# A new order of pieces for a four-part transformer kernel, with an earlier start of batch 0's query rows and paired expert products

## What is computed

```python
x = x + L0_attn(_layernorm(x))   # 16 heads of 8, softmax over 256 keys, relative tables rel_k, rel_v clipped at +-20
x = x + L0_ffn(_layernorm(x))    # rmsnorm; per token: attention of 16 heads over each other (low-rank k, v);
                                 # rmsnorm; softmax gate over 8 experts, each one 128x128 product
x = x + L1_attn(_layernorm(x))   # rmsnorm; linear attention, 8 heads of 16, second-order Taylor features
x = x + L1_ffn(_layernorm(x))    # top-2 of 8 experts + a shared one: silu((x w1 + b1)(x w3 + b3)) w2 + b2, hidden 176
```

## Time and profile before

| | us |
|---|---|
| median of 3 runs (all: 812.59, 813.42, 817.56) | 813.42 |
| the profiled execution | 821.41 |
| its span, first to last instruction | 819.6 |
| PE busy in it | 671.8 (82%) |
| DVE busy | 567.0 (69%) |
| ACT busy | 393.2 (48%) |
| POOL busy | 153.0 (19%) |
| mean granted clock of PE | 0.937 |

### The profile page before, as it was taken

How to read it: one execution, slowest core, us unless ns; L and a number is a source line. 1 busy time by engine, 2 the same in 40 slices (tenths; PEclk the granted TensorE clock), 3 DMA queues, 4 the chain that set the end, 5 groups by cost and what they waited for, 6 DMA issues and landing times.

```text
span 819.6 us, 16984 instructions
## 1 busy us (share of the span) xinstructions
PE 671.8 (82%) x6432; PEld 532.3 (65%) x6432; DVE 567.0 (69%) x1482; ACT 393.2 (48%) x953; POOL 153.0 (19%) x179
## 2 busy tenths in 40 slices
PE   2377772887799899989998999889998995877886
PEld 1256651775587678767886688668876773656655
DVE  3122178458876997699769985998589857787174
ACT  1164333544565556555556555665565453324241
POOL 2311120412040205030403041202221102011000
PEclk9998885999799999999999999999999999699799
DMA  2701100110011001100110011001100010000000
GB/s 69 253 2 14 14 7 0 15 16 7 1 15 15 7 1 21 15 7 2 20 15 8 1 20 16 8 1 21 15 1 2 8 14 0 2 7 0 1 8 6
DMA packets 75958, 13.45 MB, mean 16 GB/s; under 512 B 69851, under 2 KB 74981, under 8 KB 75749
## 3 DMA queue, kind: packets, MB, share of 16 engines
q1 hardware_dynamic: 75314, 10.84, 7.4%
q0 software_dynamic: 384, 1.05, 0.4%
q10 hardware_dynamic: 180, 0.48, 0.2%
...
## 4 chain that ended last, share of the span: by engine, by line
PE 39%; issue 34%; DVE 12%; ACT 6%; POOL 3%; SPq 3%; DMA 2%; POOLq 0%; ACTq 0%
PE bank L1026 5%; PE bank L1047 4%; PE bank L1224 4%; PE bank L1065 3%; PE bank L1225 3%; PE bank L1145 3%; DVE nmx L725 2%; PE bank L1089 2%; PE bank L1036 2%; ACT pm L451 2%; POOL q3h L602 2%; PE bank L1178 1%; SPq L373 1%; SPq L349 1%; PE bank L965 1%
## 5 line engine op out<-in xcount | busy, mean ns | idle before, releaser
L451 ACT ACTIVATE pm<-bank,nmx 128x256 f32<-128x256 f32 x256 | 100.5, 475 | 126.3 <-DVE nmx L725 126.3
L725 DVE TENSOR_REDUCE nmx<-bank 128x2 f32<-128x512 f32 x128 | 82.3, 684 | 72.7 <-PE bank L1036 72.6
L1047 PE MATMUL bank<-w,pm 128*128 128x128 f32 x512 | 84.5, 291 | 29.6 <-ACT pT L459 24.4
L1026 PE MATMUL bank<-kT,qbd 64*64 64x256 f32 x1024 | 90.7, 417 | 13.2 <-issue 12.9
L459 ACT ACTIVATE pT<-bank 128x512 f32<-128x512 f32 x128 | 77.2, 603 | 38.1 <-PE bank L1047 37.9
L1047 PEld LDWEIGHTS bank<-w,pm 128*128 128x128 f32 x512 | 63.7, 151 | 42.7 <-ACT pm L451 30.5
L934 DVE SCALAR_TENSOR_TENSOR hu<-bank,w,ha 128x256 f32<-128x256 f32 x104 | 50.1, 482 | 53.3 <-ACT ha L516 52.9
L1065 PE MATMUL bank<-tv,pT 128*128 128x128 f32 (+1 forms) x512 | 84.7, 284 | 0.0
L1065 PEld LDWEIGHTS bank<-tv,pT 128*128 128x128 f32 x512 | 75.0, 202 | 3.5 <-issue 2.1
L516 ACT ACTIVATE ha<-bank,w 128x256 f32<-128x256 f32 x104 | 49.7, 478 | 55.1 <-PE bank L1225 54.2
L1224 PE MATMUL bank<-xfT,w 128*128 128x256 f32 x208 | 66.6, 402 | 8.5 <-DVE hu L934 8.5
...
## 6 DMA issues: line engine op xcount, KB each, us to landing
...
```

Source lines behind the costliest of these rows:

```text
L451: a = act.activation(pm[:, s % 2, c, j], b_s[c][:, j * S:(j + 1) * S], exp, bias=nmx[:, i:i + 1])
L725: v.tensor_reduce(nmx[:, i:i + 2], b_s[c][:].rearrange("p (j k) -> p j k", j=2), AX_X, ALU.max, negate=True).then_inc(max_ready[0], 1)
L1026: mm(b_s[c][cols:cols + P // 2, j * S:(j + 1) * S], qbd[rows:rows + P // 2, i], kT[rows:rows + P // 2, t % 2, u], start=True, stop=False, ...
L1047: a = nc.tensor.transpose(b_t[:, (j * 2 + kc) * P:(j * 2 + kc + 1) * P], chunk(pm[:, s % 2, c, j], kc), ident)
```

## The change

- batch 0's row projection of q goes into bank b_b ahead of q^T and k^T, DVE adds its bias in project0, and v goes into b_a without waiting for kT;
- relkT and relv are loaded first; DVE fills only ek, ahead of norm0, and ACT fills ev; SP makes eight shifted copies (three before d_ev, five after), and one transfer copies them to the other 64 partitions; ACT issues the second half of qc for batch 0, DVE makes one of the first two qr blocks, and w's second part waits for qc;
- moments uses bn_aggr; tanh and the product behind it take two chunks at a time (the last one alone);
- x1 has two buffers, lsum shares lmx and y shares xl;
- every piece but the scores has a new position, and the order is computed by a sort (DRIFT is 0).

```diff
+HPAIRS = (NCH + 1) // 2
...
-PREPARE_AT = [-337, -315, -287, -256, -179, -62, 15]
+PREPARE_AT = [-352, -331, -274, -259, -93, 0, 12]
...
-ATTENTION_AT = [0, 60, 120, 180, 240, 300, 360, 420, 41, 65, 93, 109, 168, 184, 194, 254, 257, 281, 347, 358, 406, 428, 438,
-                454, 70, 129, 155, 184, 202, 232, 258, 273, 319, 345, 375, 395, 429, 444, 463, 466, 188, 296, 404, 468, 213,
-                74, 485, 501, 528, 543, 537, 548, 553, 579]
+ATTENTION_AT = [0, 60, 120, 180, 240, 300, 360, 420, 29, 74, 103, 142, 175, 185, 206, 225, 272, 278, 336, 379, 399, 416, 434,
+                446, 122, 128, 180, 191, 209, 219, 245, 245, 313, 315, 396, 408, 424, 440, 457, 463, 191, 289, 416, 467, 55,
+                24, 471, 491, 525, 550, 535, 551, 572, 585]
...
-FEED_AT = [589, 609, 611, 639, 652, 660, 663, 667, 670, 674, 680, 682, 685, 690, 690, 695, 701, 704, 714, 723, 723, 733,
-           734, 736, 736, 749, 761, 767, 768, 827, 852, 877, 905, 926, 973, 1005]
+FEED_AT = [585, 592, 602, 611, 626, 643, 652, 662, 664, 670, 673, 673, 673, 684, 699, 704, 707, 713, 718, 740, 741, 743,
+           759, 774, 781, 813, 816, 840, 855, 882, 907, 910, 920, 946, 958, 963]
...
-SECOND_AT = [1031, 1044, 1076, 1147, 1153, 1164, 1169, 1175, 1176, 1196, 1206, 1214, 1215, 1215, 1215, 1218, 1218, 1224,
-             1246, 1252]
+SECOND_AT = [974, 1031, 1059, 1088, 1112, 1141, 1156, 1173, 1175, 1177, 1192, 1220, 1221, 1227, 1236, 1257, 1268, 1274,
+             1303, 1358]
...
-LATE_AT = [1282, 1307, 1308, 1350, 1396, 1419, 1443, 1454, 1470, 1492, 1511, 1546, 1552, 1591, 1613, 1617, 1621, 1644,
-           1650, 1676, 1688, 1697, 1727, 1743]
+LATE_AT = [1360, 1366, 1378, 1392, 1408, 1427, 1436, 1442, 1475, 1527, 1555, 1579, 1597, 1630, 1638, 1657, 1659, 1660,
+           1675, 1701, 1733, 1760, 1800, 1812]
...
+DRIFT = 0
+STEP = [PERIOD + (DRIFT if k >= len(PREPARE + ATTENTION) else 0) for k in range(len(ALL))]
 PIECES = sorted([(at, k, piece) for k, (piece, at) in enumerate(zip(ALL, ALL_AT))])
+TURNS = [(t, piece) for _, _, _, t, piece in sorted([(t * STEP[k] + at, at, k, t, piece) for at, k, piece in PIECES for t in range(B)])]
...
-        x1 = sb("x1", P, C, E)
+        x1 = sb("x1", P, 2, C, E)
...
-        lsum = sb("lsum", P, C, H0)
+        lsum = lmx
...
-        y = sb("y", P, C, E)
+        y = xl
...
+        def own_rows(half):
+
+            src = bass.AP(d_qdh.tensor, half * D0, [[H0, QI * D0], [QI * D0 * H0, RT], [1, D0]])
+            return qc[half * QI * D0:(half + 1) * QI * D0], src
...
-            sp.wait_ge(rel_filled[0], 1)
-            for half in range(2):
-                for qi in range(QI):
-                    p0 = (half * QI + qi) * D0
-                    sp.dma_start(tk[p0:p0 + D0, :], ek[0:D0, QI - 1 - qi:QI - 1 - qi + TKN]).then_inc(tk_in[0], 16)
-            sp.wait_ge(rel_filled[0], 2)
+            def shifted(first, last):
+
+                for qi in range(first, last):
+                    sp.dma_start(tk[qi * D0:(qi + 1) * D0, :], ek[0:D0, QI - 1 - qi:QI - 1 - qi + TKN]).then_inc(tk_in[0], 16)
+
+            sp.wait_ge(ek_filled[0], 1)
+            shifted(0, 3)
+            sp.wait_ge(ev_filled[0], 1)
             sp.dma_start(d_ev.rearrange("m d -> (m d)").rearrange("(a n) -> a n", a=1)[:, TV0 * D0:], ev[0:1, TV0 * D0:]).then_inc(ev_out[0], 16)
+            shifted(3, QI)
             sp.wait_ge(ev_out[0], 16)
...
+                if t == 0:
+                    sp.wait_ge(tk_in[0], 16 * QI)
+                    sp.dma_start(tk[QI * D0:], tk[0:QI * D0]).then_inc(tk_copied[0], 16)
                 sp.wait_ge(*raised(qdh_out, t, 16))
                 sp.wait_ge(*raised(qr_ready, t, 0))
-                for half in range(2):
-                    src = bass.AP(d_qdh.tensor, half * D0, [[H0, QI * D0], [QI * D0 * H0, RT], [1, D0]])
-                    sp.dma_start(qc[half * QI * D0:(half + 1) * QI * D0], src).then_inc(qc_in[0], 16)
+                if t == 1:
+                    sp.wait_ge(qr0_ready[0], 1)
+                for half in range(2 if t else 1):
+                    sp.dma_start(*own_rows(half)).then_inc(qc_in[0], 16)
...
+            sp.wait_ge(qc_in[0], 32)
...
-            act.dma_start(r[:], rpack.partition_broadcast(P)).then_inc(r_in[0], 16)
             act.dma_start(ek[0:D0, S - REL + QI - 1:S + REL + QI], relkT).then_inc(rel_in[0], 16)
             act.dma_start(ev[0:1, (S - 1 - REL) * D0:(S + REL) * D0], relv).then_inc(rel_in[0], 16)
+            act.dma_start(r[:], rpack.partition_broadcast(P)).then_inc(r_in[0], 16)
             act.dma_start(b2s[:], b2).then_inc(small_in[0], 16)
...
+            def fill_ends():
+
+                act.wait_ge(rel_in[0], 32)
+                lo, hi = S - 1 - REL, S + REL
+                act.activation(view(hu, TV0 * D0, [[D0, lo - TV0], [1, D0]], 0, 1), view(hu, lo * D0, [[0, lo - TV0], [1, D0]], 0, 1), copy)
+                act.activation(view(hu, hi * D0, [[D0, EV - hi], [1, D0]], 0, 1),
+                               view(hu, (hi - 1) * D0, [[0, EV - hi], [1, D0]], 0, 1), copy).then_inc(ev_filled[0], 1)
...
+                        act.wait_ge(qdh_out[0], 16)
+                        act.dma_start(*own_rows(1)).then_inc(qc_in[0], 16)
...
-                    if 1 <= n <= NCH:
-                        act.wait_ge(*raised(u_ready, t, n))
-                        act.wait_ge(*raised(hid_ready, t, n - 2))
-                        act.activation(ht[:, (n - 1) % 2], hu[:, n - 1], ACT.Tanh).then_inc(tanh_ready[0], 1)
+                    if 2 <= n < NCH and n % 2 == 0 or n == NCH:
+
+                        k = (n - 1) // 2
+                        m = min(2, NCH - 2 * k)
+                        act.wait_ge(*raised(u_ready, t, 2 * k + m))
+                        act.wait_ge(*raised(hid_ready, t, k))
+                        act.activation(ht[:, 0:m], hu[:, 2 * k:2 * k + m], ACT.Tanh).then_inc(tanh_ready[0], 1)
...
-                    for c in range(C):
+                    for c in range(C if t or n else 1):
...
+                                        view(half_mask, 0, [[0, QI], [0, D0], [1, QI]]), ALU.mult).then_inc(qr_ready[0], 1 if t or n else C)
...
-                dve.wait_ge(tk_in[0], 16 * 2 * QI)
+                dve.wait_ge(tk_copied[0], 16)
...
-                v.tensor_tensor(mv[:], st[:, :, 1:3], st[:, :, 4:6], ALU.add)
-                v.tensor_tensor(st[:, :, 0], st[:, :, 1], st[:, :, 4], ALU.subtract).then_inc(steps[0], 1)
+                for c in range(C):
+                    a = v.bn_aggr(mv[:, c], st[:, c])
+                a.then_inc(steps[0], 1)
                 dve.wait_ge(*raised(steps, t, 2))
-                v.tensor_scalar(mv[:, :, 0], mv[:, :, 0], 0.5, None, ALU.mult)
-                v.scalar_tensor_tensor(st[:, :, 3], st[:, :, 0], E / 4, st[:, :, 0], ALU.mult, ALU.mult).then_inc(steps[0], 1)
-                dve.wait_ge(*raised(steps, t, 3))
-                v.tensor_tensor(mv[:, :, 1], mv[:, :, 1], st[:, :, 3], ALU.add).then_inc(steps[0], 1)
-                dve.wait_ge(*raised(steps, t, 4))
-                return v.tensor_scalar(ve, mv[:, :, 1], 1 / E, LN_EPS, ALU.mult, ALU.add)
+                return v.tensor_scalar(ve, mv[:, :, 1], LN_EPS, None, ALU.add)
...
+                elif name == "project0":
+                    if t == 0:
+                        dve.wait_ge(qd0_ps[0], 1)
+                        v.tensor_tensor(qdh[:], b_b[:, 0:C * E].rearrange("p (c e) -> p c e", c=C), rbc("bq_dh", C), ALU.add).then_inc(qdh_ready[0], 1)
+                        rel_tables()
                 elif name == "split0":
+                    b_v = b_p if t else b_a
                     dve.wait_ge(*raised(v_ps, t, 1))
-                    dve.wait_ge(*raised(qdh_out, t, 0))
-                    v.tensor_tensor(qdh[:], b_p[:, 0:C * E].rearrange("p (c e) -> p c e", c=C), rbc("bq_dh", C), ALU.add).then_inc(qdh_ready[0], 1)
+                    if t:
+                        dve.wait_ge(*raised(qdh_out, t, 0))
+                        v.tensor_tensor(qdh[:], b_p[:, 0:C * E].rearrange("p (c e) -> p c e", c=C), rbc("bq_dh", C), ALU.add).then_inc(qdh_ready[0], 1)
                     dve.wait_ge(*raised(v_ready, t, 0))
                     dve.wait_ge(*raised(v_off_ready, t, 0))
-                    v.tensor_tensor(vraw[:], b_p[:, C * E:2 * C * E].rearrange("p (c e) -> p c e", c=C), rbc("bv", C), ALU.add).then_inc(vraw_ready[0], 1)
+                    v.tensor_tensor(vraw[:], b_v[:, C * E:2 * C * E].rearrange("p (c e) -> p c e", c=C), rbc("bv", C), ALU.add).then_inc(vraw_ready[0], 1)
                     if t == 0:
-                        rel_tables()
+                        dve.wait_ge(*raised(qc_in, 0, 32))
+                        i = RTC
+                        v.tensor_tensor(view(qr, i * P // 2, [[P // 2, QI], [QI, D0], [1, QI]]),
+                                        view(qc, i * D0, [[D0, QI], [1, D0], [0, QI]]),
```

(31 more changed lines are left out.)

62 lines of the change are left out of this document (29 added, 33 removed).

## The result

The changed kernel took 769.62 us (median of 4 runs, 766.50 to 772.51) against 815.05 for the kernel before beside it: a ratio of 0.9442, 95% interval [0.9388, 0.9495], 45 us less. In a second comparison (g2_changed_again) the same kernel gave 0.9408 [0.9349, 0.9466].

The account below looks back on a forecast made before the run. PE was taken to bound the five full periods (92% busy), chains of waits the two ends. Terms -9.0 + 2 - 6 - 2 - 2.5 - 4 + 0 = -21.5 us, off the 813.42 median: 792.0, range 778 to 807.

Parts of the forecast that it names:

- Start: Up to PE's first score: earlier d_qdh, two queues for qc and two engines for qr gain 9.0 us, bounds 6 and 11.
- Batch 0's stage: Batch 0's attention: weigh 0 ahead of the next batch's first scores delays them, +2 us, bounds 0 and +6.
- Batch 1's stage: Batch 1's period: scores 5 ahead of the mix_scale to scale2 chain shortens the gap between maxima, -6 us, bounds 0 and -9.
- Batch 2's stage: Batch 2's period: the same as in batch 1's stage with PE better filled, -2 us, bounds +3 and -5.
- Shorter DVE and ACT work: bn_aggr and paired tanh products: DVE has 2.6 us less per period, hidden where PE is busy; -2 in the sum.
- Five full periods: PE-bound middle periods: spread chains remove some waits and add others, -0.5 us per period, -2.5 in five; bounds -25, +15.
- my own sign of being wrong: The forecast is wrong if full periods are over 84 or under 81 us.
- Rival 4: The change does more: half of PE's short waits vanish in the five periods, -15 for -2.5, 779 us; chance 0.12.
- Drain: Last batches: v's copy precedes down and batch 6's chunks fill taylor(7)'s waits, -4 us, bounds -12 and +8.
- rival 2: The 69 units deeper pipeline is paid in full in the drain, 12 us on top, 804 us; chance 0.10.
- Rival 1: Only the front gains; PE-bound periods have no slack and batch 1's gain is paid back, 804.4 us; chance 0.22.
- Rival 3: Query rows come late for scores 0, costing PE 4 us at each of seven boundaries, 820 us; chance 0.06.

Follow-up runs that it names:

- e3: The kernel before with only the changed start, the second x1 buffer and the aliases; old order, old moments, single tanh products: 803.62 us, ratio to before 0.9863.
- e4: The changed kernel with the start of the kernel before, everything else as changed: 780.28 us, ratio to before 0.9595.
- g3: The changed kernel with weigh 0 and 1 back at 485 and 501, behind the next batch's first scores: 781.11 us, ratio to before 0.9572.
- h1: The changed kernel with mix_sum3, mix_scale, turn_mix, out1, root2 and scale2 bunched ahead of scores 5 again: 808.70 us, ratio to before 0.9938.
- e1: The changed kernel with all five position lists put back to the old ones; start, bn_aggr, paired tanh and buffers as changed: 805.48 us, ratio to before 0.9896.
- e2: The changed kernel with the old six small operations in moments and single tanh products; order, start and buffers as changed: 779.64 us, ratio to before 0.9594.

## Why the prediction was wrong, point by point

**Start: right.** -9.0 forecast, -10.9 seen, 11 to 12 us by e3 and e4. Mis-sized was the time before the shifts (relkT landed by 3.12 us; 4.5 taken). On the two-engine part the trace has 1.51 us for GpSimd's block beside DVE's, where a block on GpSimd alone had taken 1.05. Both were done 1.6 us after the first began, near the 1.74 of one behind the other (0.69 and 1.05) and not the 1.2 of both at once, and the score came 1.8 us after qc. So of the two values weighed, 1.05 and 1.75, the higher is nearer. The rule of the Trainium skill ("SBUF — State Buffer", section "SBUF: two separate sides"), that one of the two engines holds the shared port pair for its whole instruction, gave 1.75: the trace agrees with it.

**Batch 0's stage: sign wrong.** +2 stood on weigh 0 delaying the next scores. With the two weighs late again (g3) the stage has 64.7 us against 65.4, so that delay is worth under 1 us here, and g3's periods show that it isn't what counts. The -5.5 seen is not the order's either: e3, with the old order, has 65.4 us in this stage too, and e4, with the new order and the old start, 64.0. It is probably nothing of the change: h2, the kernel before with only the two weighs moved, has 65.1 us from its first score to x1 of batch 0, where the profile of before has 71.0. In that profile some 10 us in the middle (60 to 70 us) ran at a mean granted clock of 0.66; h2 has 1.00 there, and e3, e4 and the changed kernel show 0.83 to 1.00 in each 10 us of that middle part. There is only one profile of before, so what lowered its clock there, and how often that happens, stays open.

**Batch 1's stage: right**, -5.6 for -6, and so is the mechanism: the gap between the maxima of quads 4 and 5 is 7.1 us, and 14.0 again in h1. **Batch 2's stage: mis-sized.** "With PE better filled: -2" should have been -4.3 for the mix chain alone (h1), and 2 more for weigh's place (g3: 77.2 against 75.2), as far as single steps taken back may be added.

**Shorter DVE and ACT work: sizes right, worth wrong.** moments to ve takes 0.96 us for 1.42, as taken; the pair's product 0.68 for the 0.69 taken. "PE's work hides this" holds in the old order (e1 against e3), not in the new one: 12 us, 6.3 of them in the five periods, where this term had 0. I had written down what the loss of the cover would cost, up to 2.6 us per period, and counted 0, though my own next step removed cover.

**Five full periods: the step that failed.** The new order alone is worth 9.4 us there (e2), with the shorter work 15.7, where I had 2.5 and 0. "Gone: the 0.5 us waits for o3T and v and hb" were three of ten kinds. The score squares, the largest row, q3h, hh and onT went too, 12.7 us in five periods; the new waits came to 11.0 rather than 6.5. The net of the waits was -11.4 us where I had -2.5. The bounds (-25, +15) held it, the range of the whole did not; my own sign of being wrong, periods under 81 us, shows in their average of 80.2. Rival 4, half of PE's short waits gone, had -15 here against -15.7 seen, and got 0.12. It named the right mechanism for this stage, but its number is in part luck: the waits fell by a third (11.4 of 31.6 us) and not by half. At 779 it was still too high, mostly since batch 2's stage gained as well.

**Drain: close in number**, -3.3 for -4 (rival 2 would have had +8), but the agreement is no evidence. Two profiles of the same kernel have 135.0 us at a granted clock of 0.88 and 127.9 at 0.95 from x1 of batch 7 to the end, where before has 138.3: a gain of 3 or of 10.

```profile
635.70:770.70 135.00, 104.81 (x548) 77.16 (x546) 84.46 (x226) 42.11 (x95) 11.63 (x14) 0.88 0.01 4
```

```profile
634.30:762.20 127.90, 97.07 (x548) 72.43 (x546) 84.17 (x226) 42.00 (x95) 11.62 (x14) 0.95 0.01 4
```

Rival 1, only the front gains, had the price of the front right: e3, which keeps the order and the computation of before, takes 803.6 us for its 804.4. It falls because the rest took off another 34. Rival 3, query rows late, shows nowhere: PE has no wait for qr in the full periods.
